# Split weights on two engines: Pool on the high parts, VectorE on the low parts, with three small edits at the kernel's head and seams

## What is computed

```python
# recurrence, 1024 steps:  xp = x @ Wx + b
next_h = tanh(xp_t + prev_h @ Wh)
# FFN on h, 2048 tokens, width 256, hidden 1024
shared = silu(h @ shared_w1.T) @ shared_w2.T
gates  = softmax(top_2(h @ gate_w.T))                  # two of eight experts
selected = sum_e gates[e] * (silu(h @ w1[e].T) @ w2[e].T)
out = x + shared + selected
```

## Time and profile before

| | us |
|---|---|
| median of 3 runs | 381.51 (381.47 to 382.41) |
| the profiled execution | 381.38 |
| its span, first to last instruction | 379.7 |
| TensorE busy in it | 356.2 (94%) |
| ScalarE | 244.1 (64%) |
| VectorE | 200.2 (53%) |
| GpSimd | 108.5 (29%) |

### The profile page before, as it was taken

One profiled execution on the slowest core, in us unless ns is written; L12 is line 12 of the kernel. 1 busy time (PEld: TensorE's weight loads), 2 busy tenths in 40 slices (PEclk: granted clock), 3 DMA queues, 4 the chain that ended last, 5 costly groups with the idle time before them and its releaser, 6 DMA issues.

```text
span 379.7 us, 8904 instructions
## 1 busy us (share of the span) xinstructions
PE 356.2 (94%) x2458; PEld 253.0 (67%) x2459; DVE 200.2 (53%) x415; ACT 244.1 (64%) x478; POOL 108.5 (29%) x99
## 2 busy tenths in 40 slices
PE   5989999997997998999999999999999999999981
PEld 4758889964664675666667666667766666666660
DVE  0089999979996988964333323333323333232310
ACT  3777788888556778865555665556665556665530
POOL 1100010000276788600123333223333133332241
PEclk9999999999999999999999999999999999999996
DMA  6999999607697979999898998889988989989992
GB/s 194 422 421 434 428 407 334 194 4 124 87 199 182 225 180 226 235 194 196 176 129 153 168 155 155 147 149 156 158 149 154 148 142 158 148 159 147 152 127 28
DMA packets 158173, 73.50 MB, mean 194 GB/s; under 512 B 140736, under 2 KB 155200, under 8 KB 156992
## 3 DMA queue, kind: packets, MB, share of 16 engines
q1 hardware_dynamic: 146672, 59.83, 66.9%
q0 software_dynamic: 6864, 9.11, 16.9%
q10 hardware_dynamic: 4608, 4.20, 4.1%
HBM read 23.68 MB, written 16.53 MB: 106 GB/s over the span
## 4 chain that ended last, share of the span: by engine, by line
PE 80%; ACT 6%; DMA 5%; issue 3%; DVE 2%; another core or an unknown queue 1%; ACTq 1%; POOL 0%; SPq 0%; DVEq 0%; POOLq 0%
PE py L1138 32%; PE z L1033 30%; PE z L1047 8%; PE z L982 3%; PE z L1014 3%; DMA space<-recurrence_w 2%; DMA space<-space 2%; ACT space L799 1%; ACT space L876 1%; PE px L1025 1%; PE py L982 1%; PE z L995 1%; DMA space<-x_cols 1%; ACTq L896 1%
## 5 line engine op out<-in xcount | busy, mean ns | idle before, releaser
L1138 PE MATMUL py<-w_slots,space 128*128 (+1 forms) x1272 | 148.4, 273 | 7.4 <-DMA space<-recurrence_w 3.7
L1033 PE MATMUL z<-w_slots,x 128*128 (+1 forms) x636 | 145.9, 379 | 0.8 <-issue 0.8
L1138 PEld LDWEIGHTS py<-w_slots,space 128*128 128x128 f16 x1272 | 123.8, 98 | 33.1 <-issue 3.5
L1033 PEld LDWEIGHTS z<-w_slots,x 128*128 128x128 f16 x636 | 62.1, 98 | 65.0 <-issue 1.2
L453 POOL DMA_INDIRECT out<-space x37 | 57.5, 1553 | 157.0 <-issue 65.2
L876 ACT ACTIVATE space<-z,tile_scales 128x512 f32<-128x512 f32 x106 | 71.8, 678 | 41.3 <-PE z L1033 34.1
L582 DVE SCALAR_TENSOR_TENSOR recurrence_w<-space,tile_scales,recurrence_w 128x512 f16<-128x512 f32 x54 | 40.5, 750 | 71.7 <-ACT recurrence_w L881 65.6
L582 DVE SCALAR_TENSOR_TENSOR space<-space,tile_scales 128x512 f16<-128x512 f32 x52 | 39.0, 750 | 57.7 <-ACT space L881 42.4
L528 DVE SCALAR_TENSOR_TENSOR w_slots<-w_slots,w_scale 128x1024 f16<-128x1024 f32 x36 | 46.2, 1283 | 1.3 <-issue 0.3
L881 ACT ACTIVATE recurrence_w<-space,tile_scales 128x512 f16<-128x512 f32 x54 | 39.0, 722 | 8.7 <-ACT space L876 2.5
L430 POOL DMA_INDIRECT sorted_rows<-space x32 | 39.1, 1221 | 17.5 <-issue 13.1
(11 more groups left out here) (114 smaller groups left out, 178.9 us busy)
## 6 DMA issues: line engine op xcount, KB each, us to landing
w_slots<-weights SPq DMA_DIRECT2D x9, 2048.0 KB, 30.5
sorted_rows<-pad_row SPq DMA_DIRECT2D x1, 5070.0 KB, 60.2
space<-x_rows ACTq DMA_DIRECT2D x16, 128.0 KB
out<-space ACTq DMA_DIRECT2D x16, 128.0 KB
space<-x_cols SPq DMA_DIRECT2D x1, 1024.0 KB, 8.6
space<-recurrence_w SPq DMA_TRANSPOSE x54
space<-space SPq DMA_TRANSPOSE x52
x<-sorted_rows SPq DMA_TRANSPOSE x39
```

The costliest lines, as they stand in the source:

```text
L1033: last = nc.tensor.matmul(Z[u % 2][h][:], x16[:, u, x_part, k], weight(f, k * HID + h * BANK, BANK, part), start=k == 0 and x_part == 0 an ...
L1138: last = nc.tensor.matmul(PY[p][:, 0:D], hiddenT[:, p, low, q], weight(f, MATRIX + q * D, D, part), start=q == 0 and not low and part == 0 ...
```

## The change

- Splits: of pieces 0 to 27 (`EARLY_WIDES` = 7 * WIDES, FFNs 0 to 6) the high part is a `tensor_scalar` on GpSimd (`split_high`), the low part stays on VectorE (`split_low`), which waits for `high_by_pool`. GpSimd waits for the scales of a batch (`scaled`) and, from piece 2 on, for the low part of piece c - 2 (`split_ok >= c - 1`); input and output now lie three slots apart (`AHEAD_SLOTS`), so that GpSimd may be one piece further. Batches are FFNs 0-1, 2, 3-4, 5-6, 7-8. The remaining eight pieces are split behind tiles 6 to 13, high part by ScalarE, low part by VectorE; the two splits at tile 3 are gone.
- Bounds: VectorE finds those of FFNs 4 and 5 too, behind the low parts of pieces 11 and 15 (`GAP_FINDS`). ScalarE's finds in the second exact round are of 512 columns (FFNs 6, 7).
- TensorE runs `WARM_UP` = 14 matmuls of `ones` by `ones` ahead of its first projection; `ones` is set first on GpSimd.
- wx, bias, wh and h0 are issued by ScalarE, the rest by SyncE.
- The last tanh of a round writes column 0 of `states` itself; the copy `next_start` and `start_ok` are gone.

```diff
-EARLY_WIDES = 6 * WIDES - 2
-BOUND_BATCHES = ((0, 2), (2, 3), (3, 4), (4, 5), (5, 6), (6, FFNS))
+AHEAD_SLOTS = 3
+WARM_UP = 14
+EARLY_WIDES = 7 * WIDES
+BOUND_BATCHES = ((0, 2), (2, 3), (3, 5), (5, 7), (7, FFNS))
+GAP_FINDS = {11: FOUND_BY_DVE + L // CHUNKS, 15: FOUND_BY_DVE + L // CHUNKS + 1}
+LATE_FINDS_FROM = max(GAP_FINDS.values()) + 1
+FOUND_BEFORE = (None, CHUNKS, 2 * CHUNKS, 3 * CHUNKS, 4 * CHUNKS + WIDES)
+BOUNDS_BEFORE = (2, 2, 3, 4, 4)
...
         def _(sp):
-            sp.dma_start(wx_sb, wx).then_inc(wx_in, 16)
...
-                if n == 0:
-                    sp.dma_start(bias_sb[:], bias).then_inc(bias_in, 16)
-                    sp.dma_start(wh_sb, wh).then_inc(wh_in, 16)
-                    sp.dma_start(states[:, :, 0, 0:B], h0_cols).then_inc(h0_in, 16)
...
         def _(pool):
+            nc.gpsimd.memset(ones[:], 1.0).then_inc(consts, 1)
...
+                pool.wait_ge(bound_ok, BOUNDS_BEFORE[n])
+                if n:
+                    pool.wait_ge(found, FOUND_BEFORE[n])
...
-            for n in range(len(BOUND_BATCHES) - 1):
+            def split_high(c):
+
+                whole, high, low, scale = wide(c)
+                if c >= 2:
+                    pool.wait_ge(split_ok, c - 1)
+                nc.gpsimd.tensor_scalar(high, whole, scale, None, ALU.mult).then_inc(high_by_pool, 1)
+
+            for n, (first, end) in enumerate(BOUND_BATCHES[:-1]):
                 reduce_bounds(n)
+                pool.wait_ge(scaled, n + 1)
+                for f in range(first, end):
+                    pool.wait_ge(w_in[f], 16)
+                for c in range(first * WIDES, end * WIDES):
+                    split_high(c)
             reduce_bounds(len(BOUND_BATCHES) - 1)
...
-            def split(c, high_by_act=False):
+            def split_low(c, ready, count):
 
                 whole, high, low, scale = wide(c)
                 if c:
                     dve.wait_ge(split_ok, c)
-                if high_by_act:
-                    dve.wait_ge(high_ok, highs_by_act.index(c) + 1)
-                else:
-                    link(nc.vector.tensor_scalar(high, whole, scale, None, ALU.mult))
+                dve.wait_ge(ready, count)
                 nc.vector.scalar_tensor_tensor(low, whole, scale, high, ALU.mult, ALU.subtract).then_inc(split_ok, 1)
...
+            for n, (first, end) in enumerate(BOUND_BATCHES[:-1]):
                 find_scales(n)
-                split_upto(min(BOUND_BATCHES[n][1] * WIDES, EARLY_WIDES))
+                dve.sem_inc(scaled, 1)
...
+                for c in range(first * WIDES, end * WIDES):
+                    split_low(c, high_by_pool, c + 1)
+                    if c in GAP_FINDS:
+                        find_largest(GAP_FINDS[c]).then_inc(bound_ok, 1)
...
-                    for c in LATE_SPLITS[g - SPLIT_FROM]:
-                        split(c, high_by_act=c in highs_by_act)
+                    split_low(EARLY_WIDES + g - SPLIT_FROM, high_by_act, g - SPLIT_FROM + 1)
...
         def _(act):
+            nc.scalar.dma_start(wx_sb, wx).then_inc(wx_in, 16)
+            nc.scalar.dma_start(bias_sb[:], bias).then_inc(bias_in, 16)
+            nc.scalar.dma_start(wh_sb, wh).then_inc(wh_in, 16)
+            nc.scalar.dma_start(states[:, :, 0, 0:B], h0_cols).then_inc(h0_in, 16)
...
-                        nc.scalar.activation(column(m, i * 2 + u + 1), Z[p][m][:, u * COLS:(u + 1) * COLS], ACT.Tanh).then_inc(h[m], 1)
-                    if starts_next and u == 1:
-                        next_start(r + 1, states[:, :, L])
+                        if starts_next and u == 1:
+                            nc.scalar.activation(next_start(m), Z[p][m][:, u * COLS:(u + 1) * COLS - B], ACT.Tanh).then_inc(h[m], 1)
...
         def _(pe):
+            pe.wait_ge(consts, 1)
+            for _ in range(WARM_UP):
+                nc.tensor.matmul(PX1[:, 0:P], ones[:], ones[:], start=True, stop=True)
             pe.wait_ge(wx_in, 16)
```

More of the change, by code:

```diff
@@ L87 @@
 RING = 4
-SPACE = 2 * K * NTOK + 2 * HID - 512
+SPACE = 2 * K * NTOK + HID
 AHEAD = 2
@@ L288, in weight @@
             return w_split[:, bass.ds(f * (2 * WCOLS) + (2 * c + part) * WIDE + start, n)]
-        highs_by_act = [late[0] for late in LATE_SPLITS]
         def wide(c):
@@ L295, in wide @@
             high, low = (w_split[:, (2 * c + part) * WIDE:(2 * c + part + 1) * WIDE] for part in range(2))
-            return w_slots[:, 2 * c + 2:2 * c + 4].rearrange("p s c -> p (s c)"), high, low, w_scale[:, f, m:m + 1]
+            return w_slots[:, 2 * c + AHEAD_SLOTS:2 * c + AHEAD_SLOTS + 2].rearrange("p s c -> p (s c)"), high, low, w_scale[:, f, m:m + 1]
         x_tiles = x_rows.rearrange("(t p) d -> t p d", p=P)
@@ L385, in _ @@
             nc.gpsimd.memset(pad_row[:], 0.0).then_inc(pad_ok, 1)
-            nc.gpsimd.memset(ones[:], 1.0).then_inc(consts, 1)
             pool.wait_ge(identity_ok, 2)
@@ L523, in split @@
                     dve.wait_ge(split_ok, c)
-                if high_by_act:
-                    dve.wait_ge(high_ok, highs_by_act.index(c) + 1)
-                else:
-                    link(nc.vector.tensor_scalar(high, whole, scale, None, ALU.mult))
+                dve.wait_ge(ready, count)
                 nc.vector.scalar_tensor_tensor(low, whole, scale, high, ALU.mult, ALU.subtract).then_inc(split_ok, 1)
-            def split_upto(end):
-                for c in range(split_done[0], end):
-                    split(c)
-                split_done[0] = end
-            split_done = [0]
             for f in range(FOUND_BY_DVE):
@@ L778, in _, with next_start @@
             act.wait_ge(bias_in, 16)
+            def next_start(m):
+                return states[:, m, 0, B:COLS]
             def project_out(i, m):
@@ L793, in _ @@
                         act.wait_ge(z_mm[m], i * 2 + (u + 1))
-                        nc.scalar.activation(guess[:, 1 - u, m], ahead[i % 3][m][:, u * COLS:(u + 1) * COLS], ACT.Tanh,
-                                             bias=bias_sb[:, m:m + 1]).then_inc(h_ok[m], 1)
+                        if i * 2 + u + 1 == L:
+                            nc.scalar.activation(next_start(m), ahead[i % 3][m][:, u * COLS:(u + 1) * COLS - B], ACT.Tanh,
+                                                 bias=bias_sb[:, m:m + 1]).then_inc(h_ok[m], 1)
+                        else:
+                            nc.scalar.activation(guess[:, 1 - u, m], ahead[i % 3][m][:, u * COLS:(u + 1) * COLS], ACT.Tanh,
+                                                 bias=bias_sb[:, m:m + 1]).then_inc(h_ok[m], 1)
             def find_bound(c, n):
-                nc.scalar.activation(magnitudes[:, 0:n * CHUNK], w_slots[:, bass.ds(c + 2, n), :].rearrange("p a c -> p (a c)"), ACT.Abs,
+                nc.scalar.activation(magnitudes[:, 0:n * CHUNK], w_slots[:, bass.ds(c + AHEAD_SLOTS, n), :].rearrange("p a c -> p (a c)"), ACT.Abs,
                                      accum_out=chunk_bound[:].rearrange("p f c -> p (f c)")[:, bass.ds(c, 1)]).then_inc(found, 1)
@@ L803, in find_last, with step_pair @@
                 find_bound(LAST * CHUNKS + 2 * c, 2)
-            def next_start(r, ends):
-                for k in range(K):
-                    act.wait_ge(h_ok[k], r * L)
-                act.sem_inc(act_waited, 1)
-                nc.scalar.copy(states[:, :, 0, B:COLS], ends[:, :, 0:COLS - B]).then_inc(start_ok, 1)
-            def step_pair(z, h, r, i, p, find_at=None, chunks=1, starts_next=False):
+            def step_pair(z, h, r, i, p, find_at=None, starts_next=False):
                 for u in range(2):
@@ L931, in _ @@
                     c = WIDES // 2 + g - 1
-                    act.wait_ge(found, found_upto(LAST) + c)
+                    act.wait_ge(found, 4 * CHUNKS + c)
                     find_last(c)
                 if SPLIT_FROM <= g < TILES - 2:
-                    c = highs_by_act[g - SPLIT_FROM]
+                    c = EARLY_WIDES + g - SPLIT_FROM
                     whole, high, low, scale = wide(c)
-                    act.wait_ge(split_ok, c)
-                    nc.scalar.mul(high, whole, scale).then_inc(high_ok, 1)
+                    act.wait_ge(scaled, len(BOUND_BATCHES))
+                    act.wait_ge(split_ok, c - 1)
+                    nc.scalar.mul(high, whole, scale).then_inc(high_by_act, 1)
                 if g > AHEAD:
@@ L1038, in pair @@
             def pair(z, h, r, i, p, first=False, final=False, route=False):
+                chained = isinstance(r, int) or not first
                 for u in range(2):
                     for k in range(K):
-                        if k == 0 and not (first and u == 0):
+                        if k == 0 and (chained or u):
                             pe.wait_ge(h[0], i * 2 + (r * L + u))
                         for m in range(K):
-                            if k + m == 1 and not (first and u == 0) and (m == 1) == (u == 1):
+                            if k + m == 1 and (chained or u) and (m == 1) == (u == 1):
```

66 lines of the change are left out of this document (26 added, 40 removed).

## The result

The changed kernel takes 465.7 us (median of 4 runs, 465.32 to 466.44) against 381.96 for the kernel before (4 runs, taken beside it): ratio 1.2155, 95% interval 1.2098 to 1.2211. It is slower by some 84 us, where the prediction said 24 and its range ended 40 above. The profiled execution took 465.3 us with a span of 463.6.

The account below looks back on a forecast made before the run. The FFN stage's start, waiting for VectorE's early splits, was taken to set the time: 381.4 + 25.6 (later splits) + 0.5 (clock) - 2.5 (relief) = 405.0 us, range 378 to 421.

Parts of the forecast that it names:

- E: End of VectorE's early splits, ahead of the first FFN matmul: from 79.7 to 105.3 us, + 25.6, paid in full.
- Start of the finds: Head of the kernel: VectorE's finds start near 16.8 us, not 18.1; the second ends at 26.1, not 27.43.
- The price of a high part: One 1024-column high part on GpSimd before the FFN stage: 1.0 us, bounds 0.93 and 2.2, above 1.5 unlikely.
- Turns: Early splits: GpSimd's highs and VectorE's lows alternate at SBUF, 2.36 us a piece, 66.1 us for 28 pieces.
- What stands between batches: Among the early splits: finds + 6.8, scales + 4.6, reduces and wake-ups + 1.7 us.
- rival D: Early splits: turns with a slow GpSimd high of 1.5 us, + 14, 419 us; a 7.84 us stall possible too; chance 0.12.
- Relief behind 92: FFN stage, 92 to 150 us: lighter VectorE work takes back 2.5 us, between 0 and 4.5.
- The clock: Start of the FFN stage: TensorE, idle some 26 us before, starts at half speed; + 0.5 us, at most 2.
- The small parts: Warm-up, two queues and tanh into column 0, all ahead of the early splits' end: 0 us on the path.
- B: Early splits: highs run beside lows but still end late, + 3.3 us; 382.2 to 384.7 us; chance 0.15.
- C: Highs beside lows, with FFN-stage relief removing 4.5 to 7.1 us: 380.2 to 377.6 us; chance 0.20, 0.15 of it faster.
- Rival E: Head: the change doesn't do what it says, warm-up only keeps TensorE from the projections; + 1.4 us at most; no separate chance.

## Why the prediction was right and wrong

*E sets the time at full price.* Right. E moved by 83.4, the start of the FFN stage by 83.4, the time by 83.9. With the highs on VectorE E moved by 25.0 and the profiled time by 27.7, with copies by 23.0 and 26.2, and TensorE's one long wait, 17.4 and 18.1, is for the same `states_low`.

*Start of the finds.* Right: 17.12, where 16.8 was said; the second ends at 26.44 for 26.1.

*The price of a high part: 1.0 us, "above 1.5 unlikely".* This step failed. It is 2.83, outside the bounds of 0.93 and 2.2 too. The nearest rows that I took were memsets, which compute nothing; they do price a copy (1.04 measured), but the multiplying operation takes 2.5 ns a column where the copy takes about 1. Why it does is not shown by any run. The affine select that gave the upper bound is again another operation: no row priced this one. An honest upper end was open. The page's figure that I set beside it, 1.8 cycles an element (the Trainium skill, GPSIMD Engine Reference, "Elementwise — side-by-side cycle accounting"), gives an estimate of 1.54 us and is too low as well; 2.5 ns would be 3.0 cycles at its 1.2 GHz.

*Turns.* Half right, and only for short highs. With copies they are nearly as said, 2.18 us a piece where 2.36 was summed. With the real operation a low is held up by 0.79 us of 2.83, and the pace is the high's own, 2.83, not 1.28 + 2.83. The rule cited in the prediction (SBUF — State Buffer, "SBUF: two separate sides", of the Trainium skill) has the lock last for the whole instruction. The trace agrees for VectorE's low (a high begun inside it, with 1.23 us of it to go, takes 1.1 us more), nearly for GpSimd's copy (0.83 us of 1.04), and disagrees for GpSimd's `tensor_scalar`: there VectorE is free again after 0.9 us of 2.83. So the sum of the 28 pieces, 66.1, became 81.6 (80.2 and the last low): + 15.5.

*What stands between batches.* This is the larger failure: 6.8 + 4.6 + 1.7 = 13.1 us for finds, scales and reduces against 53.4 + 1.6 + 0.1 = 55.1: + 42.0. VectorE's scales and one of its two finds cost next to nothing, as they lie beside GpSimd's idleness of 5.7 to 11 us at each change of operation; the other find shows as the 2.15. The prediction saw the row (7.84 us in front of the first affine select) and named it in rival D as a stall that "would come here too", once and without a price. It comes seven times. The kernel before shows no such stretch at its reduces: the change to the first one lies under a wait for VectorE, and between its reduces GpSimd runs nothing. The Trainium skill has the size: the first call to a freshly loaded kernel pays about 6 us with no visible instruction in the profile (GPSIMD Engine Reference, "Instruction dispatch"). The trace agrees with it, 5.7 to 6.3 on the way back to the reduce and 5.9 to 9.9 from the last scale to the first high, and adds that coming back to an operation used before counts as a first call again. That the idle time is code being loaded is the page's reading; what the runs show is that it goes when the reduces go (28.9 us less idle), that it goes with copies, and that it is no matter of busy DMA queues: the last four stretches, 5.7 to 7.2 us, fall between 80 and 160, where the DMA share is 0.00. Why the first one is longer (11.04, and 10.24 in the run without the later reduces) is open: the DMA share is 1.01 beside it, but 1.09 beside the 6.27.

With 0.3 for the start, 0.3 + 15.5 + 42.0 = 57.8 makes 105.3 into 163.1.

*Relief behind 92: 2.5 us.* Wrong, there is none to be seen: from E to the end the profiled executions take 302.2 us, 304.3 with the highs on VectorE and 304.8 with copies, against 301.6 before. TensorE works 63.34 us of 68 from 172 to 240, 4.7 idle, as the 4.54 of the earlier trace rows, and waits 1.7 us for VectorE's line 592, the former 598, where it was 2.0.

*The clock, 0.5 us.* The granted clock was 0.54 from 80 to 160, mostly its lower level (1.2 GHz), with TensorE idle from 83.2 on, and 0.69 from 160 to 172; the first six FFN matmuls took 2.72 us for 1.46, which alone is 1.3 us.

*The small parts, 0.* Right on the changed kernel's path, since GpSimd is so much later. But not right in themselves: the two queues, "worth 0.4 us" if anything, let h0 land 9.4 us behind its issue instead of 3.1, and make the kernel before 1.5 to 2.9% slower. I had counted the issues that leave SyncE's queue and not asked how the other queue is served next to it. The warm-up was as said: 28 cold instructions in 6.26 us, projections at full speed from 7.15.

*The rivals.* B and C needed highs beside lows, which came true in part, at a pace that made it worthless. D had the right signs, a slow high and a stall, and less than half of their size: 38 us against the 84. Rival E's + 1.4 doesn't show either: the warm-up costs nothing.

## What to carry to other kernels

Price an operation that moves to GpSimd from a row of that very operation, not from memsets or copies: here 2.83 against 1.04 us for the same bytes. Look at its neighbours on GpSimd too: going from a reduce to `tensor_scalar` and back cost 12.8 to 14.2 us, where a batch of four pieces saved VectorE 4 x 0.754 = 3.0. And moving work in front of a seam where an engine is only just in time is paid in full (some 27 of the 84 us stay when GpSimd has no high parts). Before all that, compare the pace: a piece in turns, 2.18 us even with a copy, is no faster than VectorE's own 2.11.

## What was not expected of the hardware

- GpSimd's `tensor_scalar` on 128 x 1024 f32: 2.83 us, 2.5 ns a column and 0.28 fixed; a converting copy 1.04.
- Each change between the cross-partition reduce and `tensor_scalar` on GpSimd: 5.7 to 11 us idle, a pair of MODIFY_POOL_CONFIG in front of it; none with copies.
- A two-input VectorE operation of 1.28 us beside it stands still only until 0.9 us behind the start of the 2.83 us; beside a copy of 1.04 until 0.83 (it then takes 2.14).
- A load of 2 KB at the end of ScalarE's queue: 9.4 us to land, against 3.1 from SyncE's queue ahead of the large loads.
- The first affine select of GpSimd, idle 7.84 us before, came later still with the inputs on two queues; in GpSimd's timeline of the changed kernel:

```profile
15.22 0.28 POOL L378 TENSOR_SCALAR_AFFINE_SELECT identity<-identity 128x128 f32<-128x128 f32 x1 [13.68 <-issue]
```

All runs agree: 7.2 to 8.3 us in the five kernels with one input queue, 11.4 to 13.7 in the seven with two. So the stretch grows with the second queue, as h0's does; what it waits for is not shown.
